# Attention stage of a fused attention and mixture-of-experts layer: the hi and lo copies of the transposed rows one half pair earlier

## The reference

```python
xn = _layernorm(x, axis=-1)
x = x + attention(xn) + ffn(xn)

# attention: window of 128 behind each query
scores = jnp.einsum('bqhd,bkhd->bhqk', q, k) * SCALE
scores = jnp.where((j <= i) & (j >= i - 128), scores, -10000.0)
attn = softmax(scores) + 1e-09
ctx = einsum('bhqk,bkhd->bqhd', attn, v);  out = ctx @ Wo.T + bo

# ffn: routed experts, and a shared expert on all rows
sh = silu(xn @ shared_gate_w) * (xn @ shared_up_w)
out = combined + sh @ shared_down_w
```

## Time and profile before

| | us |
|---|---|
| median of 3 runs | 1661.37 (1661.45, 1661.37, 1656.77) |
| the profiled execution | 1655.14 |
| its span | 1653.4 |
| TensorE matmuls, busy in the span | 1520.1 (92%) |
| VectorE | 1105.7 (67%) |
| ScalarE | 979.6 (59%) |
| GpSimd | 1109.0 (67%) |
| a turn, start to start (turns 3 to 15) | 44.3 to 44.8 |

### The profile page before, as it was taken

One profiled execution on the slowest core, in us unless ns is written; L12 is line 12 of the kernel. 1 busy time (PEld: TensorE's weight loads), 2 busy tenths in 40 slices (PEclk: granted clock), 3 DMA queues, 4 the chain that ended last, 5 costly groups with the idle time before them and its releaser, 6 DMA issues.

```text
span 1653.4 us, 38959 instructions
## 1 busy us (share of the span) xinstructions
PE 1520.1 (92%) x11382; PEld 1252.6 (76%) x11382; DVE 1105.7 (67%) x3788; ACT 979.6 (59%) x2043; POOL 1109.0 (67%) x1158
## 2 busy tenths in 40 slices
PE   4878868999999999999998899999999999999998
PEld 4766747998888999888997666677777777667766
DVE  7999875666666666666666566766666676666652
ACT  5767744454455455544554466666666666666664
POOL 1878775334433444434331488999999999999998
PEclk9999988999999999999999599999999999999999
DMA  6777755554555555545576477878877777788752
GB/s 195 269 269 269 286 195 184 170 165 156 162 165 168 160 170 164 162 138 176 164 245 149 89 155 159 178 167 174 172 173 163 163 155 164 165 168 176 168 133 88
DMA packets 228581, 288.89 MB, mean 175 GB/s; under 512 B 59488, under 2 KB 146144, under 8 KB 228512
## 3 DMA queue, kind: packets, MB, share of 16 engines
q1 hardware_dynamic: 170064, 207.30, 46.9%
q10 hardware_dynamic: 45488, 45.36, 9.6%
q0 software_dynamic: 12960, 35.41, 8.5%
HBM read 198.07 MB, written 79.95 MB: 168 GB/s over the span
## 4 chain that ended last, share of the span: by engine, by line
PE 58%; DVE 15%; ACT 10%; issue 8%; ACTq 4%; POOL 3%; DMA 2%; DVEq 0%; POOLq 0%
PE psum L152 33%; PE psum L970 11%; PE psum L1573 5%; PE psum L1531 4%; ACT plain_arena L1688 4%; PE psum L1554 2%; DVE split_arena L736 2%; PE psum L1157 2%; DVE plain_arena L1804 2%; ACTq L1707 1%; DVE stats L631 1%; ACTq L1708 1%; DVE split_arena L729 1%; ACT plain_arena L1702 1%; ACT plain_arena L1749 1%
## 5 line engine op out<-in xcount | busy, mean ns | idle before, releaser
L152 PE MATMUL psum<-split_arena 128*128 128x512 f32 (+2 forms) x4752 | 939.0, 350 | 12.3 <-DVE split_arena L1261 7.3
L152 PEld LDWEIGHTS psum<-split_arena 128*128 128x128 f32 x4752 | 750.3, 192 | 132.6 <-issue 22.9
L1804 DVE CUSTOM_DVE_ANT_0 plain_arena<-psum,mask 128x256 f32<-128x256 f32 (+1 forms) x1024 | 338.4, 385 | 198.0 <-PE psum L1531 194.2
L1688 ACT ACTIVATE plain_arena<-psum 128x512 f32<-128x512 f32 (+1 forms) x512 | 250.3, 541 | 201.7 <-PE psum L1554 171.9
L1120 POOL TENSOR_TENSOR split_arena<-plain_arena,split_arena 128x1024 fp32r<-128x1024 f32 x43 | 103.2, 2401 | 227.3 <-ACT split_arena L1192 227.0
L1226 ACT ACTIVATE plain_arena<-psum 128x512 f32<-128x512 f32 (+1 forms) x172 | 90.2, 525 | 249.7 <-PE psum L152 249.6
L970 PE MATMUL psum<-split_arena 128*128 128x256 f32 x1704 | 217.9, 286 | 3.5 <-DVE split_arena L1291 3.5
L970 PEld LDWEIGHTS psum<-split_arena 128*128 128x128 f32 x1704 | 208.0, 191 | 5.7 <-DVE split_arena L1291 4.1
L1296 DVE TENSOR_TENSOR plain_arena<-psum,plain_arena 128x512 f32<-128x512 f32 (+1 forms) x172 | 102.3, 595 | 139.9 <-ACT plain_arena L1226 137.6
L1112 POOL DMA_INDIRECT plain_arena<-xn_d,run_ix x142 | 137.1, 965 | 69.2 <-POOL run_ix L1109 35.2
L1448 POOL TENSOR_SCALAR_AFFINE_SELECT plain_arena<-plain_arena 128x1024 f32<-128x1024 f32 x128 | 140.5, 1098 | 39.5 <-ACT plain_arena L1688 38.7
(11 more groups left out here) (199 smaller groups left out, 1852.7 us busy)
## 6 DMA issues: line engine op xcount, KB each, us to landing
plain_arena<-in_gate_w SPq DMA_DIRECT2D x43, 512.0 KB, 3.4
plain_arena<-in_up_w SPq DMA_DIRECT2D x43, 512.0 KB, 4.1
plain_arena<-in_down_w SPq DMA_DIRECT2D x43, 512.0 KB, 3.4
plain_arena<-in_x SPq DMA_DIRECT2D x32, 512.0 KB, 7.0
q_d<-split_arena SPq DMA_DIRECT2D x32, 512.0 KB, 3.6
k_d<-split_arena SPq DMA_DIRECT2D x32, 512.0 KB, 5.1
split_arena<-q_d SPq DMA_DIRECT2D x128, 128.0 KB, 4.4
split_arena<-k_d SPq DMA_DIRECT2D x128, 128.0 KB, 4.8
```

The costliest lines, as they stand in the source:

```text
L152: last = pe.matmul(out, lhs_t(p), rhs(q), start=(begins and c == 0 and k == 0), stop=(ends and c == len(chunks) - 1 and k == 2), skip_grou ...
L1688: act.activation(b_pt[:, g % 2, 2 * p + par, 4 * half:4 * half + n, :].rearrange("p k s -> p (k s)"), psum[:, 2 + par, 0:n * P], ACT.Exp, ...
L1804: last = dve.tensor_tensor_reduce(b_junk[:, 2 * par + i % 2, 0:cols], psum[:, par, at:at + cols], mask[:, 2 * P - cols:2 * P], -1.0, 3e38, ...
```

## The change

In `b_scalar`'s and in `b_vector`'s turn the calls of `rows_hi` and `rows_lo` move from half pairs 4 and 5 to half pairs 3 and 4. Nothing else moves: TensorE, GpSimd and SyncE have the same instructions in the same order.

```diff
@@ b_scalar, turn
-                    if h in (4, 5) and valid(t - 1):
-                        rows_hi(t - 1, h - 4)
+                    if h in (3, 4) and valid(t - 1):
+                        rows_hi(t - 1, h - 3)
@@ b_vector, turn
-                    if h in (4, 5) and valid(t - 1):
-                        rows_lo(t - 1, h - 4)
+                    if h in (3, 4) and valid(t - 1):
+                        rows_lo(t - 1, h - 3)
```

## The result

| | before | after |
|---|---|---|
| median of 20 runs each, same chip, us | 1661.41 | 1667.05 |
| profiled execution, us | 1655.14 | 1664.4 |
| its span, us | 1653.4 | 1662.7 |

After to before is 1.0034 (95% interval 1.0023 to 1.0045): the change costs 5.6 us. The forecast was 1661 us and no measurable difference. The time lies inside the range of 1652 to 1669, but the whole interval lies above 1, so "no measurable difference" does not hold. The profiled executions are one of each kernel, 6.3 us under the median for before and 2.7 under it for after; times inside a turn are read from them, and the price of the change from the medians.

A forecast was written before the change was run, and what follows sets the result against it. TensorE's matmuls were taken to fill nearly the whole turn; +0.6 us over 14 turns, 0 in turn 1 and -0.4 in turn 16 gave +0.2, so 1661 us, own range 1655 to 1666, full range 1652 to 1669.

The forecast's parts named there:

- Rival 1: ScalarE's first copy starts before the second transfer's issue ends, so the gain comes through: 12 us faster, 1649 us; chance 0.11.
- Rival 3: Five hand-overs between engines up to the value sums each cost 0.1 us more: 7 us slower, 1668 us; chance 0.08.
- +0.04 a turn: Value sums of half pair 6 start at 1129.27 instead of 1129.23, +0.6 us over 14 turns.
- the 1.2 us forecast for it: TensorE's scores of half pair 5 wait 1.2 us for half pair 4's reductions, replacing 0.87 us before the maxima's transposes.
- Rival 2: Copy of the maxima, issued 0.74 us later, lands too late for half pair 8: 10 us slower, 1671 us; chance 0.07.
- turn 16: The 0.79 us gap before the value sums goes, later exponentials push transposed scores some 0.4: -0.4 us left.
- the queues passed: Transfers issued later, the maxima's copy and SyncE's store of reciprocals (0.5 us later, needed in half pair 9), cost nothing.
- the point to compare: Start of the value sums in half pair 6: afterwards TensorE runs on by itself, so what moves it moves the turn.

The follow-up runs named there:

- e5: The changed kernel with the store of the output moved from ScalarE's queue to SyncE's: 1679.34 us, 1.0052 of the kernel before.
- e6: The kernel before with the store of the output moved from ScalarE's queue to SyncE's: 1675.35 us, 1.0036 of the kernel before.
- e7: Kernel before with ScalarE's copies in half pairs 3 and 4, and VectorE's subtraction ahead of the reciprocals in half pair 5: 1664.24 us, ratio 0.9972.
- e1: Kernel before with SyncE's store of the first chunk's reciprocals also waiting for the second subtraction: 1673.27 us, 1.0095 of the kernel before.
- e13: The changed kernel with the load of normalised rows issued for the first sequence alone: 1655.91 us, 0.9974 of the kernel before.
- e14: The kernel before with the load of normalised rows issued for the first sequence alone: 1654.43 us, 0.9962 of the kernel before.
- e2: Kernel before with only ScalarE's copies moved to half pairs 3 and 4, VectorE's subtractions left: 1654.45 us, 0.9979 of the kernel before.
- e3: Kernel before with only VectorE's subtractions moved to half pairs 3 and 4, ScalarE's copies left: 1735.23 us in one run.
- e4: The changed kernel with the load of normalised rows moved from half pair 8 to half pair 12: 1661.25 us, 1.0041 of the kernel before.

## Why the prediction was wrong

**Right, ScalarE.** In us after L1737, measured with the prediction in brackets: copy of c = 0 4.19 (4.23), exponentials 4.68 (4.76), copy of c = 1 5.95 (6.04). It started 0.04 behind the end of the second issue (1129.14 + 0.55 to 1129.73): an issue of 0.55 us holds ScalarE's work. Rival 1 falls with this row. The Trainium skill, page "DMA: Bandwidth & Descriptors", section "Issuing engines are not separate DMA queues", calls the time of an issue usually small beside the transfer. That agrees with this trace, 0.55 us against a median of 4.6 from issue to landing for this transfer of 128 KB in before; the prediction read more into it, that the work behind the issue would hardly be held, and this does not follow and did not happen. The same section says that transfers started by different engines run on the same 16 DMA engines. That agrees with e5 and e6, where another queue relieved nothing.

**Right, VectorE.** Subtractions at 4.81 and 6.58 (4.85, 6.66), reductions at 5.42 and 7.19 (5.46, 7.27), reciprocals at 8.57 (8.64). Rival 3 falls: the hand-overs cost what I read, or up to 0.1 less.

**Right, TensorE.** Transposes of the maxima at 7.27 (7.25), transposed scores of half pair 6 at 8.94 (9.00), value sums at 9.36 (9.33). The forecast for these half pairs was +0.04 a turn, and they measured +0.07 there and +0.08 as a mean. The wait changed its place, one step ahead, as worked out; of the 1.2 us forecast for it 0.67 is a wait that the trace names, and the rest lies inside the `scores`, which take 1.06 us from first start to last end instead of 0.51, bank by bank.

**Right, the copy of maxima that Rival 2 names.** Half pair 8 kept its length (2.58, 2.59). The mechanism of Rival 2, a copy of maxima that lands too late, is however the one that cost the time, in another half pair and from another cause: not by its issue, but by the traffic around it.

**Right but without effect, turn 16.** Its value sums came 1.36 us earlier after L1737, where I had taken 0.4, yet the last matmul of the program starts 92.0 us after the first `scores` of turn 15 against 91.9 before. The -0.4 of the sum should have been 0.

**Wrong: the queues passed.** The step that failed is "The reciprocals' store in SyncE's queue comes 0.5 later and its result is needed in half pair 9, so nothing". The 0.5 was nearly right (8.57 against 8.15 us after L1737 for the reciprocals; the spreading is 0.6 later), and nothing in half pair 9 waits for its result. I asked who waits for the result of the store and not who waits for the DMA engines. With it fell the sentence that the start of the value sums in half pair 6 is the point to compare, that "what moves it moves the turn": in e7 it came 1.06 us earlier and half pair 12 gave 0.7 back. What the runs showed in its place is +0.19 us a turn in half pairs 12 and 13 (0.38 less 0.19). e1 shows that the late store and spreading alone lengthen half pair 12, and e13 with e14 that the price is gone when the stretch ahead of it isn't full. Over 14 turns the terms are 0.08 x 14 = 1.1 us (forecast 0.6), 0.19 x 14 = 2.7 and for half pair 9 0.08 x 14 = 1.1, together 4.9; the other half pairs take 0.3 off, and 0.33 x 14 = 4.6 are left of the 5.6 us measured. In the prediction these last two stood at 0.

**Open.** The +0.08 of half pair 9 comes from turns 4, 7 and 9 to 13 (2.35 to 2.58 instead of 2.27); in the last five SyncE idles 0.5 to 0.7 us around the start of half pair 8 and VectorE 0.4 behind it, while TensorE's matmuls have no gap. It is gone in e13, which names the load of rows or its timing as a condition and not a mechanism, and it isn't there in e1 (2.27), so the later spreading alone doesn't make it. The 1.0 us that the sum leaves, and turn 1's 2.7 us in the profile with its stretch at half clock, were not tested apart; over the 20 runs of after, the time goes with the granted clock (correlation -0.82). How a later spreading turns into a later landing of the copy is argued from the traffic, and its size is not settled: the spreading is 0.6 later in after and the gap 0.4 longer, and 1.1 and 0.8 in e1. From one turn to the next of one kernel the gap differs by more than that, for no cause that was looked for.

## What to carry to other kernels

When an instruction is delayed, follow its transfer and every transfer behind it in its queue, and look at the DMA share of the stretch in which they now fall: a small copy on the path of the matmuls can pay for a full stretch, though nobody waits for the delayed data. Look too at what the next step gives back: here the first 1.0 us of the gap was free. Where two engines hand a value over, moving only the producer early (ScalarE's copy) kept the gain, and moving the in-order consumer too (VectorE's subtraction) gave it to the reductions behind it. Put bulk loads into the stretch in which the DMA engines are idle, and measure it together with the change that they limit.

## What the runs showed of the hardware

- The same copy of maxima took 4.5 us from issue to use in before's half pair 12 and 4.9 in after's (3.63 + 0.86 and 3.62 + 1.24), and 9.0 in the longest wait of e2 (3.63 + 5.38, turn 2). With a DMA share of 0.30 in the 2 us before (e14, turn 5) the gap was 0.33, that without a wait; with 1.12 it was 1.63 (after, turn 5). The share alone does not decide: e3 has 0.93 as a mean and a gap of 0.33.
- Putting a store into another engine's queue moved its issue by 1.7 to 2.2 us and made the kernel slower (e5, e6).
- An issue of a transfer of 0.55 us on ScalarE held the copy behind it until 0.04 us after its end (after, turn 5).
- A late copy can cost more than its own wait. Where a gap in half pair 12 was followed by one stretch at half clock, half pairs 12 and 13 took 1.42 to 1.50 us more than the gap explains (14 turns, gaps of 1.73 to 3.33). Other gaps as long had no such stretch behind them (2.31 in turn 9 of e5, 3.22 in turn 2 of e4).
